# Sliding-window attention with an int8 gate on 8 cores: the K transpose of each chunk issued in two halves

## The reference, cut to what matters

```
xn = layernorm(x)                                   # over 1024 features
q, k, v = xn @ Wq.T, xn @ Wk.T, xn @ Wv.T           # 16 heads of 64
s = softmax(q @ k2.T / 8, banded) @ v2              # chunks of 128 queries; k2, v2: the chunk before and this one
s = s @ Wo.T
qx = round(xn / sx);  qr = round(rhs / sr)          # int8 by row of xn, by column of rhs
g = silu((qx @ qr) * sx * sr)
y = x + s * g
```

## Time and profile before

| | us |
|---|---|
| median of three runs | 839.24 |
| the profiled execution, its time | 839.21 |
| span of its slowest core (core 4) | 837.7 |
| spans of the eight cores | 833.6 to 837.7 |
| TensorE matmul busy | 658.5 (79%) |
| VectorE busy | 528.1 (63%) |
| ScalarE busy | 420.2 (50%) |
| queue q1, all of SyncE's DMAs: share of 16 engines' span | 49.2% |
| DMA transposes in the loop | 192, 3.1 to landing |

### The profile page before, as it was taken

The page is one execution under the profiler, slowest core; times in us unless marked ns, Lnnn a source line. Parts: engine busy times, 40 slices in busy tenths (PEclk is TensorE's granted clock), DMA queues, the critical chain, the costliest instruction groups (busy, mean ns, idle before and its releaser), DMA issues.

```text
span 837.7 us, 13584 instructions; the slowest of 8 cores (833.6 to 837.7 us)
## 1 busy us (share of the span) xinstructions
PE 658.5 (79%) x4561; PEld 343.7 (41%) x4625; DVE 528.1 (63%) x1083; ACT 420.2 (50%) x481; POOL 17.6 (2%) x36
## 2 busy tenths in 40 slices
PE   0001579888988988889898898898888989888984
PEld 0001234444444444444444444444444444444442
DVE  4544156666666676667666666667666766666633
ACT  0001255565555666555555555566655555655641
POOL 8000000000000000000000000000000000000000
PEclk9999999999999999999999999999999999999996
DMA  9999356446566544565555545555545565446421
GB/s 175 187 214 169 80 76 114 102 94 109 89 114 113 112 103 98 105 110 106 113 114 99 94 91 109 114 108 100 110 100 112 105 113 113 97 96 102 74 63 63
DMA packets 194066, 91.29 MB, mean 109 GB/s; under 512 B 180296, under 2 KB 180680, under 8 KB 194000
## 3 DMA queue, kind: packets, MB, share of 16 engines
q1 hardware_dynamic: 188816, 79.95, 49.2%
q0 software_dynamic: 4608, 8.39, 6.4%
q10 hardware_dynamic: 576, 2.10, 0.9%
HBM read 37.98 MB, written 16.78 MB: 65 GB/s over the span
## 4 chain that ended last, share of the span: by engine, by line
DVE 35%; PE 31%; DMA 14%; issue 13%; ACT 3%; SPq 2%; DVEq 1%; ACTq 0%
PE p_proj L527 18%; PE p_av L627 14%; DMA bfp<-bfp 9%; DVE bfp L349 6%; DVE scr L394 4%; DVE sm L259 4%; DVE scr L405 4%; DVE sm L247 4%; DMA scr<-rhst 3%; DVE scr L385 3%; DVE scr L253 2%; DVE bfp L362 2%; DMA scr<-x 1%; SPq L161 1%; DVE sm L315 1%
## 5 line engine op out<-in xcount | busy, mean ns | idle before, releaser
L527 PE MATMUL p_proj<-wbf,bfp 128*128 128x512 bf16 x1473 | 336.0, 381 | 72.2 <-DMA bfp<-bfp 23.4
L527 PEld LDWEIGHTS p_proj<-wbf,bfp 128*128 128x128 bf16 x1536 | 144.3, 98 | 234.2 <-issue 83.9
L627 PE MATMUL p_av<-wbf,bfp 128*128 128x512 bf16 x511 | 117.1, 382 | 24.3 <-DMA bfp<-bfp 21.5
L497 ACT ACTIVATE scr<-scr 128x1024 f32<-128x1024 f32 x32 | 33.8, 1057 | 185.8 <-DVE scr L385 185.8
L527 PE MATMUL p_proj<-qrhs,bfp 128*128 128x512 bf16 x512 | 115.7, 379 | 1.1 <-ACT bfp L482 1.1
L627 PEld LDWEIGHTS p_av<-wbf,bfp 128*128 128x128 bf16 x512 | 48.0, 98 | 92.8 <-issue 41.3
L381 DVE SCALAR_TENSOR_TENSOR scr<-p_proj,sm,scr 128x512 f32<-128x512 f32 x32 | 24.0, 751 | 91.2 <-PE p_proj L527 91.2
L467 ACT ACTIVATE q32t<-scr,sm 128x1024 int32<-128x1024 f32 x32 | 36.8, 1149 | 85.0 <-DVE bfp L325 66.6
L349 DVE TENSOR_TENSOR bfp<-bfp,mstd_s 128x2048 bf16<-128x2048 bf16 x60 | 71.1, 1222 | 9.7 <-DVE scr L253 4.7
L527 PEld LDWEIGHTS p_proj<-qrhs,bfp 128*128 128x128 bf16 x512 | 50.1, 98 | 61.7 <-issue 1.5
L544 PE MATMUL p_sc<-bfp 128*128 128x128 bf16 x512 | 64.8, 220 | 3.8 <-ACT bfp L429 3.8
(11 more groups left out here) (63 smaller groups left out, 758.9 us busy)
## 6 DMA issues: line engine op xcount, KB each, us to landing
scr<-x SPq DMA_DIRECT2D x32, 512.0 KB, 5.9
y<-scr SPq DMA_DIRECT2D x32, 512.0 KB, 3.9
bfp<-bfp SPq DMA_TRANSPOSE x192, 3.1
scr<-rhst ACTq DMA_DIRECT2D x4, 512.0 KB, 8.2
wbf<-wqt POOLq DMA_DIRECT2D x8, 256.0 KB, 14.8
scr<-rhst SPq DMA_DIRECT2D x4, 512.0 KB
wbf<-wkt POOLq DMA_DIRECT2D x8, 256.0 KB, 26.4
wbf<-wvt POOLq DMA_DIRECT2D x8, 256.0 KB, 38.1
```

The source lines that it names most:

```text
L497: I(lambda c=c: scalar.activation(scr[:, GS[c % 2]:GS[c % 2] + 1024], scr[:, GPRE:GPRE + 1024], AF.Tanh, scale=0.5), "a", ("silu", c))
L527: mms.append(lambda kc=kc, half=half: tensor.matmul(p_proj[:, half * 512:(half + 1) * 512], lhs_t[:, lhs_base + kc * 128:lhs_base + kc * 1 ...
L627: mms.append(lambda kc=kc, half=half, c=c: tensor.matmul(p_av[:, half * 512:(half + 1) * 512], bfp2[:, AOT[c % 2] + kc * 128:AOT[c % 2] + ...
```

## The change

The one transpose of K for a chunk becomes two of four blocks each, and so two of 128 x 512 instead of one of 128 x 1024. The first waits for kte0 alone and counts on a new semaphore (trka); the second waits for kte and keeps the old one (trk). TensorE waits for trka ahead of SCORES(i, 0), and for trk ahead of SCORES(i, 1). Nothing else moves: the two stand where the one stood in SyncE's order, and the bytes transposed are the same.

```diff
+                    ap4k = lambda off: bass.AP(bfp, off, [[BFP_COLS, 128], [128, 4],
+                                                           [1, 128]])
+                    W(sync, "a", ("kte0", c))
+                    I(lambda c=c, ap4k=ap4k: sync.dma_start_transpose(
+                        ap4k(KT[c % 2]), ap4k(KROW)),
+                      f"trka{c % 2}", ("trka", c), 16)
                     W(sync, "a", ("kte", c))
-                    I(lambda c=c: sync.dma_start_transpose(
-                        ap3(bfp, BFP_COLS, KT[c % 2]), ap3(bfp, BFP_COLS, KROW)),
+                    I(lambda c=c, ap4k=ap4k: sync.dma_start_transpose(
+                        ap4k(KT[c % 2] + 512), ap4k(KROW + 512)),
                       f"trk{c % 2}", ("trk", c), 16)
...
                 if 0 <= i < nchunk:
                     W(tensor, "a", ("qtm", i))
-                    Wv(tensor, f"trk{i % 2}", 16 * (i // 2 + 1))
+                    Wv(tensor, f"trka{i % 2}", 16 * (i // 2 + 1))
                     if i >= 1:
                         W(tensor, "v", ("ao", i - 1))
                     SCORES(i, 0)
...
                 if 0 <= i < nchunk:
                     W(tensor, "a", ("e0", i))
+                    Wv(tensor, f"trk{i % 2}", 16 * (i // 2 + 1))
                     SCORES(i, 1)
```

More of the change, by code:

```diff
@@ L110, in build @@
         sem_names = (["ldw", "ldw2", "st", "v", "a", "t", "trs", "lwq", "lwk", "lwv", "lwo"]
-                     + [f"{k}{p}" for k in ("trxn", "trql", "trq", "trk", "trao",
-                                            "traoa")
+                     + [f"{k}{p}" for k in ("trxn", "trql", "trq", "trk", "trka",
+                                            "trao", "traoa")
                         for p in (0, 1)]
```

## The result

The changed kernel takes 840.66 us (median of 28 runs, 839.07 at the fastest), the kernel before 839.58 us beside it. A few runs, two here and four there, were slow ones of 856 to 909 us, in which a program on eight cores now and then runs whatever the kernel; ratios and means leave such runs out. The ratio is 1.0018, with a 95% interval of 1.0010 to 1.0025: 1.5 us slower, 0.8 to 2.1. That is within the 0.3% called no change, and inside the range of 836.3 to 842.9, but clear of zero. The profiled execution took 839.68 us.

The account below looks back on a forecast made before the run. The prediction took the ring through VectorE, traoa, the output projection and ffn, 22.50 us a period, as the bound; K's transpose isn't in it. Its three parts summed 0 + 0 + 0 to 839.2 us, range 836.3 to 842.9.

Parts of the forecast that it names:

- Part 1: First half of K's transpose: lands 1.3 us before the whole did, 3.9 us before its reader; gain 0.
- the path: The ring of waits through VectorE, traoa, output projection and ffn that sets the period of 22.50 us.
- Part 2: Second half of K: issued 1.28 us after the first, landing level with the old whole transpose; cost 0.
- The added wait on TensorE at 0: Wait for trk ahead of SCORES(i, 1): met long before it is reached; between 0 and 0.1 us possible, 0 taken.
- what lies around the span: Profiled execution's time beyond the slowest core's span: 839.21 against 837.7 us, 1.5 us.
- Part 3: Issues behind K on SyncE: trql 0.76 us later, trxn mostly unmoved, otherwise up to 0.76 later; cost 0.
- the average wait of 0.87: SyncE's wait for L300 ahead of trxn: 27 times of 32, 23.5 us in all, 0.87 each.
- The limit of 1.11 us for a late trxn: Before the Q projection: a delay below 0.51 + 0.60 us costs nothing; 1.50 in the other kind of period.
- In all 31: Claim that the shift of trql and trxn costs 0 in every one of the 31 periods.
- the slack of 0.60: On VectorE: a Q projection 1.11 us late made L362 only 0.51 late, so 0.60 us is absorbed.
- 854.7 us: Estimate by the skill page if fixed DMA parts don't overlap: trxn 2.0 us later, 0.50 us in each of 31 periods.
- The rival of the irregular periods: A few late periods fall otherwise as SyncE's issues shift: 835.5 to 842.9 us; chance 0.05 faster, 0.06 slower.

Follow-up runs that it names:

- three_pieces: The changed kernel with K in three transposes a chunk (4, 2 and 2 blocks) instead of two: 868.32 us, 1.0309 of the kernel before.
- again: The changed kernel measured once more, nothing altered: 1.0014 (1.0003 to 1.0026) of the kernel before.
- again_2: The changed kernel measured another time, on the chip of the later runs: 1.0024 (1.0005 to 1.0042) of the kernel before.

## Why the prediction was right or wrong

- Part 1, no gain on the path from an earlier K: right. No score waits for a transpose before or after, and split against whole shows nothing that stays when trql is out of the way and the wait is gone.
- Part 2, the halves' times: right (1.28 apart, 2.4 to 2.5 to landing). The added wait on TensorE at 0: wrong, and this is the step that failed. In its place in the loop it costs nothing, as the row said. What it cost is one packet more of instructions after the end, 0.8 us outside the span (2.35 instead of 1.56; 1.58 again once the wait was gone). The prediction named what lies around the span, 1.5 us, and held it constant without a reason. (That two neighbours each land in 2.4 to 2.5 us, its rows show for traoa alone; the trace has 2.4 in the median for trao too, so it holds.)
- Part 3, trql 0.76 later, trxn not: right in the median (0.77 and 0). But the average wait of 0.87 against a shift of 0.76 leaves a margin of 0.1 us, and late Q projections doubled. Their cost of 0 holds for the inner periods of the three profiled executions of the changed kernel. The limit of 1.11 us for a late trxn left out that TensorE's clock can fall behind the longer idle time, as three_pieces shows. "In all 31" is wrong: the slack of 0.60 comes from VectorE's statistics for chunk i+2, and in the last two chunks there are none.
- The DMA engines' work for two halves as for a whole: right. By the Trainium skill (DMA: Bandwidth & Descriptors, Rules for kernel authors, on coalescing small transfers) I had estimated 854.7 us; two halves don't show it. The 2.0 us in that estimate are the page's figure for DMAs that GpSimd issues, and those of this kernel are SyncE's. Three pieces do cost, but by SyncE's issue time and what is queued behind it, not by a fixed part of the transfers.
- The rival of the irregular periods was near the truth in kind (SyncE's or other traffic falls otherwise), with a chance of 0.06. What moves is TensorE's instruction packets against traoa, and I could have seen them in the queue list of the profile's page. That the time lies inside the range is this rival's width and so partly luck: the sum itself was 0.
- The inner gain of 1.2 us that hid half of the loss in the spans was in no part of it.

The parts sum to +0.8 us in the profiled executions against 1.5 (0.8 to 2.1) measured. Over all runs, the time outside the span is longer by 0.8, 0.8 and 0.7 us in the three groups of the changed kernel, so this part is firm. The slowest core's span is longer by 0.1 us in again (0.7 either way) and by 1.5 in again_2 (1.4 either way). So the spans hold the rest, it differs from group to group, and no run here settles how large it is.

## What to carry to other kernels

Before a transfer is split, look at the engine that issues it: the price of another piece is its issue time, here 1.2 us whatever the size, paid by everything queued behind it, and it is free only up to the idle time ahead of the next waiting issue, and that in each period and not on average. Past the slack, look at TensorE's granted clock as well as at the delay. Take slack from the periods at the ends of the loop as well as from its middle. And when a change is worth tenths of a per cent, count instructions too: length of stream and numbering of semaphores moved this kernel as much as the change did.

## What was not expected of the hardware

- A packet of TensorE's instructions (16 KB, queue q8) that begins 0.5 to 1.2 us behind the issue of a transpose of 128 KB delays what waits for it by 0.3 to 1.2 us (49 of 49 cores in 16 kernels); one that begins 0.3 us or more ahead of the issue doesn't (519 times). One more packet after the end adds 0.8 us to the run.
- In 34 inner periods of these 16 kernels' traces TensorE's granted clock fell to 0.50 for 3.4 us; each time TensorE had sat idle for 1.99 us or more ahead of the Q projection, and each of these periods is over 2 us too long. In 79 others with such an idle time the clock held.
- Two unused semaphores in the list moved the landing of traoa from 2.46 to 2.42 us.
- The issue of a DMA transpose takes SyncE 1.2 us for 2, 4 or 8 blocks of 128 columns.
